# Who makes the high part of the hidden tiles in a Strassen expert: two gelus on ScalarE, or one gelu and a copy on VectorE

## What is computed

```python
x = x + xattn(layernorm(x), ctx)
# experts: 8, each picks 512 tokens of each batch (top_k of its gate's softmax)
h = einsum('nekd,edf->nekf', xin, w1)      # 512 -> 2048
h = gelu(h, approximate=False)
h = einsum('nekf,efd->nekd', h, w2)        # 2048 -> 512
out = out.at[batch_idx, m].add(g[..., None] * h)
```

## Time and profile before

| what | value |
|---|---|
| median of 3 runs | 1783.54 us (1780.68 to 1787.02) |
| the profiled execution | 1785.64 us |
| its span in the profile | 1783.9 us |
| PE busy | 1724.9 us, 97% of the span |
| VectorE (DVE) busy | 1164.5 us, 65% |
| ScalarE (ACT) busy | 807.7 us, 45% |
| GpSimd (POOL) busy | 477.3 us, 27% |
| mean granted TensorE clock | 0.988 of full |

### The profile page before, as it was taken

One profiled execution on the slowest core, in us unless ns is written; L12 is line 12 of the kernel. 1 busy time (PEld: TensorE's weight loads), 2 busy tenths in 40 slices (PEclk: granted clock), 3 DMA queues, 4 the chain that ended last, 5 costly groups with the idle time before them and its releaser, 6 DMA issues.

```text
span 1783.9 us, 22943 instructions
## 1 busy us (share of the span) xinstructions
PE 1724.9 (97%) x8502; PEld 1435.8 (80%) x8502; DVE 1164.5 (65%) x1946; ACT 807.7 (45%) x1786; POOL 477.3 (27%) x451
## 2 busy tenths in 40 slices
PE   7999999899999999999999999999999999999997
PEld 6799988687787878888878887888788878887886
DVE  5455477677766665766686668666766676676663
ACT  4556656363333333544454445445444544454442
POOL 2122222210113020431254216312621361143112
PEclk9999999899999999999999999999999999999999
DMA  3233335242335242431152114312331341133003
GB/s 124 71 131 106 116 111 187 83 154 95 88 123 144 95 139 98 107 106 48 48 95 95 48 54 89 103 63 62 71 105 48 71 103 63 48 73 69 24 1 47
DMA packets 76125, 156.30 MB, mean 88 GB/s; under 512 B 4436, under 2 KB 4590, under 8 KB 76023
## 3 DMA queue, kind: packets, MB, share of 16 engines
q1 hardware_dynamic: 61687, 121.38, 19.7%
q0 software_dynamic: 14336, 33.56, 10.4%
HBM read 121.37 MB, written 33.55 MB: 87 GB/s over the span
## 4 chain that ended last, share of the span: by engine, by line
PE 77%; DVE 9%; ACT 7%; issue 6%; DMA 1%; POOL 1%; SPq 0%; DVEq 0%; ACTq 0%; POOLq 0%
PE ps L1746 7%; PE ps L1748 7%; PE ps L1747 7%; PE ps L1768 7%; PE ps L1769 7%; PE ps L1770 7%; PE ps L1652 3%; PE ps L1654 3%; PE ps L1653 3%; PE ps L1639 3%; PE ps L1641 3%; PE ps L955 3%; PE ps L1640 3%; PE ps L956 3%; PE ps L957 3%
## 5 line engine op out<-in xcount | busy, mean ns | idle before, releaser
L1768 PE MATMUL ps<-v2h,hhS 128*128 128x512 f32 x768 | 302.6, 394 | 4.9 <-DVE YS L1546 3.4
L1769 PE MATMUL ps<-v2l,hhS 128*128 128x512 f32 x768 | 299.1, 390 | 0.0
L1770 PE MATMUL ps<-v2h,hlS 128*128 128x512 f32 x768 | 299.0, 389 | 0.0
L1746 PE MATMUL ps<-Th,Wh 128*128 128x512 f32 x672 | 264.0, 393 | 13.0 <-ACT u L1355 9.2
L1748 PE MATMUL ps<-Th,Wl 128*128 128x512 f32 x672 | 263.1, 392 | 0.0
L1747 PE MATMUL ps<-Tl,Wh 128*128 128x512 f32 x672 | 263.1, 392 | 0.0
L1529 DVE TENSOR_TENSOR hlS<-hfS,hhS 128x512 fp32r<-128x512 f32 x192 | 172.3, 906 | 73.9 <-ACT hfS L1346 73.9
L1199 POOL TENSOR_TENSOR Wf<-w_raw 128x512 f32<-128x512 f32 x24 | 31.2, 1299 | 613.7 <-PE ps L1748 613.7
L1327 ACT ACTIVATE v2h<-w_raw 128x512 fp32r<-128x512 f32 x96 | 57.6, 624 | 273.7 <-PE ps L1770 273.7
L1546 DVE SCALAR_TENSOR_TENSOR YS<-ps,tok_gate,YS 128x512 f32<-128x512 f32 x144 | 105.8, 745 | 113.7 <-PE ps L1770 113.7
L1768 PEld LDWEIGHTS ps<-v2h,hhS 128*128 128x128 f32 x768 | 144.2, 188 | 41.4 <-DVE YS L1546 8.4
(11 more groups left out here) (212 smaller groups left out, 3576.7 us busy)
## 6 DMA issues: line engine op xcount, KB each, us to landing
w_raw<-in_L_ffn_w_dram SPq DMA_DIRECT2D x80, 1024.0 KB, 5.2
XB<-in_x_dram SPq DMA_DIRECT2D x16, 512.0 KB, 4.0
XR<-in_x_dram SPq DMA_DIRECT2D x16, 512.0 KB, 3.5
out_dram<-X SPq DMA_DIRECT2D x16, 512.0 KB, 4.7
xn_rows<-XN SPq DMA_DIRECT2D x16, 512.0 KB, 5.4
w_raw<-in_L_xattn_Wq_dram SPq DMA_DIRECT2D x1, 1024.0 KB, 9.6
w_raw<-in_L_xattn_Wo_dram SPq DMA_DIRECT2D x1, 1024.0 KB, 12.9
w_raw<-in_L_xattn_Wk_dram SPq DMA_DIRECT2D x1, 768.0 KB, 6.5
```

The lines of the kernel that those rows point to most:

```text
L1746: nc.tensor.matmul(ps[:, bank, :], wh, th, start=(idx in OPENS and k == 0), stop=False, **go_on)
L1768: nc.tensor.matmul(ps[:, bank, :], th, wh, start=(t == 0), stop=False)
L1769: nc.tensor.matmul(ps[:, bank, :], th, wl, start=False, stop=False)
L1770: last = nc.tensor.matmul(ps[:, bank, :], tl, wh, start=False, stop=(t == GF - 1))
```

## The change

`hidden` now applies the gelu once, into `hfS`. `low` copies `hfS` into the fp32r tile `hhS` on VectorE, waits for that copy, and then subtracts as before. A semaphore `s_high` is added for that wait. The order of all lists stays, and `low` is called in the same places.

```diff
-        (s_prod, s_u1, ..., s_gelu, s_hid, ...
+        (s_prod, s_u1, ..., s_gelu, s_high, s_hid, ...
@@ hidden(n, m), ScalarE
-                nc.scalar.activation(hhS[:, b, f], src, ACT.Gelu)
                 nc.scalar.activation(hfS[:, b, f], src, ACT.Gelu).then_inc(s_gelu, 1)
@@ low(n, m), VectorE
                 dve.wait_ge(s_gelu, ND * n + m + 1)
+                nc.vector.tensor_copy(hhS[:, b, f], hfS[:, b, f]).then_inc(s_high, 1)
+                dve.wait_ge(s_high, ND * n + m + 1)
                 nc.vector.tensor_tensor(hlS[:, b, f], hfS[:, b, f], hhS[:, b, f].bitcast(F32),
                                         ALU.subtract).then_inc(s_hid, 1)
```

More of the change, by code:

```diff
@@ L1112, in xattn_expert_choice @@
         s_raw2 = [sem(f"s_raw2_{i}") for i in range(2)]
-        (s_prod, s_u1, s_c11, s_u2, s_u7, s_c22, s_c21, s_gelu, s_hid, s_sum, s_Wh, s_Wl, s_v2h, s_v2l, s_dn, s_ev, s_tr, s_Ta,
+        (s_prod, s_u1, s_c11, s_u2, s_u7, s_c22, s_c21, s_gelu, s_high, s_hid, s_sum, s_Wh, s_Wl, s_v2h, s_v2l, s_dn, s_ev, s_tr, s_Ta,
          s_T2, s_Td, s_Th, s_Tl, s_rows, s_scat) = (sem(f"s_{n}") for n in (
-             "prod u1 c11 u2 u7 c22 c21 gelu hid sum Wh Wl v2h v2l dn ev tr Ta T2 Td Th Tl rows scat").split())
+             "prod u1 c11 u2 u7 c22 c21 gelu high hid sum Wh Wl v2h v2l dn ev tr Ta T2 Td Th Tl rows scat").split())
         def w_block(n, idx):
```

## The result

The changed kernel is slower: 1807.84 us in the median of 4 runs (1798.93 to 1815.51), against 1785.28 us (1780.68 to 1787.69) for the kernel before, now over 4 runs. The ratio is 1.0128, with a 95% interval from 1.0076 to 1.018. The two profiled executions have spans of 1807.0 and 1783.9 us, so 23.1 us are to be explained.

The account below looks back on a forecast made before the run. TensorE, busy 97% of the span, was taken as the bound, so only its waits count. Terms of +14.2, +2.2 and -2.2 us made +14.2, on the median of 1783.5 giving 1797.7 us, with a range of 1788 to 1808 us.

Parts of the forecast that it names:

- term 3: Five starts of an expert: one gelu less on ScalarE outweighs VectorE's copy before c11(1), 5 x 0.45 = -2.2 us.
- the granted clock: In one start it was 0.55 over 4 us; costed at nothing, though shorter waits may save at most some 3 us.
- Term 1: Before down chunk 3 in 18 groups, g = 0 to 2: evict(n, 0) comes 0.79 us later, +14.2 us.
- The list of turns: VectorE's tail rewritten, copies and lows alternating with GpSimd's four sums; evict(n, 0) ends at 1199.73 instead of 1198.94.
- the row: Profile row of the copy at 738.37: a copy's turn ends 0.28 us behind GpSimd's end, less than its 0.43 alone.
- Term 2: Fourth transposes in five g = 3 groups: 0.33 us lost plus some 0.1 restarting, 5 x 0.45 = +2.2 us.
- fourth rival: Clock falls to the lower level after the longer eviction waits in the 18 groups: +29 us, 1826 us; 4%.
- keep its turn past a sum: Rival at VectorE's hand-over with GpSimd: one sum falls behind evict(n, 0), -6.5 us, 1777 us; 6%.
- nearly free: Rival in VectorE's tail: copies cost only 0.28 us each, 0.22 per group, about 1787 us; 8%.
- move forward: Rival at chunk 0: low 6 misses a turn and TensorE waits there some 1.4 us, 1801 us; 15%.

Follow-up runs that it names:

- late_tiles: Changed kernel, but only tiles 5, 6 and 7 get VectorE's copy and tiles 0 to 4 get the two gelus of before: 1802.79 us, ratio to before 1.0094.
- sums_late: Changed kernel, with GpSimd's four sums for the next group waiting for evict(n, 0) where g = 0, 1 or 2: 1776.68 us, ratio to before 0.9938.
- evict_early: Changed kernel, with evict(n, 0) moved in VectorE's list in front of the next group's three w_low: 1773.92 us, ratio to before 0.9938.
- early_tiles: Changed kernel, but only tiles 0 to 4 get VectorE's copy and tiles 5, 6 and 7 the two gelus: 1778.16 us, ratio to before 0.9953.
- c11_ahead: Changed kernel, with c11(0) and c11(1) before the low parts of w2 in the first group of experts 2 to 6: 1781.47 us, ratio to before 0.9982.
- both_gelus: Changed kernel, with ScalarE also applying the second gelu into hhS, which VectorE's copy then overwrites: 1810.14 us, from one run.

## Why the prediction was right and wrong

The forecast was +14.2 us, and the profiles differ by 23.0. Two steps of it failed, and they hold 8.4 of the missing 8.8 us: term 3 (3.3 us, with the wrong sign), and the granted clock, which was costed at nothing (5.1 us).

**Term 1, the eviction (forecast +14.2, measured +14.3).** The place, the mechanism and the size held: 0.79 us per group forecast, 0.81 to 0.82 measured in most groups. The list of turns was met nearly step by step: a copy's turn was 0.29 us (0.28 forecast), and the first sum stood behind low 5 as said. `late_tiles` shows that only the three late copies count, `sums_late` that the copies fit where there are no turns, `evict_early` that it matters only because the eviction stands last.

The rule weighed there, of the Trainium skill, "SBUF — State Buffer", section "SBUF: two separate sides", gives the shared ports to whoever starts first for the whole instruction, and would have made 1.09 us of it. That two operations never ran through at once agrees. But a copy that had been issued meanwhile ended 0.29 us after GpSimd, not 0.42, so the measured 0.81 decides for the row.

**Term 2, the transposes (forecast +2.2, measured +2.5).** Right: five waits of 0.2 to 0.3 us idle, 0.5 us with restarting.

**Term 3, the starts (forecast -2.2, measured +1.1). This step failed**, by 3.3 us and in sign. I had priced ScalarE's two gelus and VectorE's copy behind `c11(0)`, and let `c11(0)` itself stand where it stood. But what holds `c11(0)` is GpSimd. VectorE's first `v2l` of the expert has two SBUF inputs and stands until the four `t_low` of GpSimd are through. The changed kernel, VectorE then GpSimd, with the first product of the group at 1091.87:

```profile
1093.16 6.71 DVE L1506 TENSOR_TENSOR v2l<-w_raw,v2h 128x512 fp32r<-128x512 f32 x1 [0.34 <-ACT v2h L1327]
...
1100.39 0.68 DVE L1512 TENSOR_TENSOR hfS<-ps,u 128x512 f32<-128x512 f32 x1
```

```profile
1090.40 2.00 POOL L1189 DMA_INDIRECT out_dram<-YS,tok_idx  x1 [0.16 <-issue]
...
1093.71 5.60 POOL L1209 TENSOR_TENSOR Tl<-Tf,Th 128x512 fp32r<-128x512 f32 x4
```

In the kernel before, where the first product starts at 1085.31:

```profile
1083.51 1.56 POOL L1189 DMA_INDIRECT out_dram<-YS,tok_idx  x1 [0.17 <-issue]
...
1086.38 5.62 POOL L1209 TENSOR_TENSOR Tl<-Tf,Th 128x512 fp32r<-128x512 f32 x4
```

The `t_low` block starts 1.07 us after the group's first product before, 1.84 after the change: 0.77 us later, and `c11(0)` with it. GpSimd's list is a chain of scatters and `t_low` behind VectorE's evictions. The link is `evict(n, 3)` of the group with g = 3 before it, which stands behind the second stage of transposes in VectorE's list, here before and after:

```profile
1075.72 0.74 DVE L1546 SCALAR_TENSOR_TENSOR YS<-ps,tok_gate,YS 128x512 f32<-128x512 f32 x1
```

```profile
1082.59 0.74 DVE L1547 SCALAR_TENSOR_TENSOR YS<-ps,tok_gate,YS 128x512 f32<-128x512 f32 x1
```

It ends 8.85 us before the next group's first product before, and 8.54 us after the change, some 0.3 us later: VectorE's delay of 0.8 us less the 0.5 us that TensorE itself lost at the transposes. The scatters behind it keep that delay (the fifth starts 1.80 and 1.47 us ahead of the first product). The other 0.44 us of the 0.77 are the fifth scatter, whose issue takes 2.00 instead of 1.56 us. So the delay that I had counted at the transposes came back through a second engine. It does not come from the waits at chunk 3: `evict_early` has none of those, its `evict(n, 3)` is as late as in the changed kernel, and its block starts at 1.84 too. `early_tiles` confirms it from the other side: GpSimd is on time there (the block starts at 1.06 to 1.09), and the start gains 0.57 us, within the 0.30 to 0.60 of the forecast. The 0.30 taken off for the scatter was not needed: the copy beside it lasted 0.43 us. `c11_ahead` shows that this hold is behind both of a start's waits.

**The clock (forecast 0, measured +5.1 in the profiled pair).** This was left at nothing, with "at most some 3 us" beside it for what shorter waits could save. It is the largest part that the sum lacked, and it carried the median to the upper edge of the range; that it stayed inside is luck, since the sum had no term for it. The changed kernel's four runs line up by mean granted clock: spans of 1797.2, 1805.3, 1807.0 and 1813.8 us at 0.99, 0.987, 0.985 and 0.98. Apart from one at the very end of each execution, all falls in the stage lie in starts, where TensorE has two waits close together. One of them, in columns as in the earlier trace rows:

```profile
1277.23:1278.73 1.50, 1.50 (x6) 1.05 (x6) 1.25 (x2) 0.22 (x1) 0.89 (x1) 1.00 0.96 146
1278.73:1285.50 6.77, 5.92 (x15) 4.56 (x15) 3.53 (x6) 3.25 (x7) 0.00 (x0) 0.50 0.78 194
```

The granted clock is 1.00 after the first wait and then 0.50 for 6.8 us, which is the level of 1.2 GHz. Such a fall costs 2.6 us (48.34 against 45.76). The prediction read the fall of the earlier trace rows as one after two waits. The traces show otherwise: each fall begins within 1.5 us after the end of the first wait, before the second one begins (here the first ends at 1277.23 and the clock falls at 1278.73). The fourth rival had put the falls at the waits for the eviction. There, none fell, in 18 waits of 1.1 us. But the two kernels in which those waits were taken away have fewer falls at the starts too (`evict_early` and `sums_late`, two and one in five, against four), so that they have no part in it is not shown.

**The other rivals.** VectorE did not keep its turn past a sum, and the copies were not nearly free. The wait did not move forward in the changed kernel; in `both_gelus`, with 0.65 us less room at the starts, it did there.

## What to carry to other kernels

An engine at 65% is no cover by itself: find the one operation in its list that the bounding engine asks for, and count what stands in front of that. A delay in one list also has to be followed into the lists that wait for it: here VectorE's delay made GpSimd late, and GpSimd's block then held VectorE. Before giving an engine more work, try the order of its list: moving three calls was worth 31 us in the kernel before, while one gelu less brought some 8 us in the best form tried here, and only for the tiles that come early.

## What the runs showed of the hardware that was not expected

- GpSimd's four `t_low` follow each other every 1.25 us, and VectorE never got a turn between them, as it does between GpSimd's sums. Its operation with two SBUF inputs ended 0.56 us after the last of the four, whether it had been issued 0.55 us ahead of the block, with a scatter's issue still under way (6.71 us in the changed kernel), 0.21 us into it (5.96 us in the kernel before) or 4.4 us into it (1.8 us in `c11_ahead`, whose block is shown below). What decides between turns and a whole block was not tried. `c11`, with one input in PSUM and one in SBUF, ran beside the same block in its usual 0.69 us.

```profile
1089.06 5.62 POOL L1209 TENSOR_TENSOR Tl<-Tf,Th 128x512 fp32r<-128x512 f32 x4
```

- The issue of a scatter on GpSimd takes 1.55 to 1.58 us, and longer where one of VectorE's operations with two SBUF inputs has begun before it (and no second one follows it at once): with 0.32, 0.56 and 0.66 us of that operation left it takes 1.75, 2.00 and 2.10 us. The added time is what is left of that operation, less some 0.12 us. That is the 2.00 at the start of an expert: after the change VectorE's `w_low` begins 0.12 us ahead of the fifth scatter (1090.28 and 1090.40), before it 0.21 us behind it (1083.72 and 1083.51), and then the scatter keeps its 1.56 us. No run was made to test this; it is read from the traces.

```profile
1083.72 0.68 DVE L1502 TENSOR_TENSOR Wl<-Wf,Wh 128x512 fp32r<-128x512 f32 x1
```

```profile
1090.28 0.68 DVE L1501 TENSOR_TENSOR Wl<-Wf,Wh 128x512 fp32r<-128x512 f32 x1
```

- The length of the waits alone does not decide whether the clock falls. `both_gelus` has the longest waits of all kernels at its starts (2.6 and 1.6 us) and no fall there. Ten microseconds around one start's waits, in the same columns:

```profile
1277.73:1287.73 10.00, 6.51 (x27) 5.11 (x28) 5.84 (x11) 6.39 (x12) 1.97 (x2) 1.00 0.65 126
```

- With waits of 2.1 and 0.9 us at five starts the changed kernel had four falls, `evict_early` two and `sums_late` one; `late_tiles` (2.6 and 0.9 us) had three. Each count is from one profile. Kernels without waits at the starts had none, and agree within 2.4 us from run to run. What sets off a fall stays open.
